# A transformer of eight stages on one core: the two-layer experts' routing done per group, partly inside the last attention slot

## The reference, cut to what matters

```python
x = x + tanh(g_xattn[2]) * L2_xattn(layernorm(x), ctx)   # stage 4: 16 heads
x = x + tanh(g_ffn[2])   * L2_ffn(layernorm(x), ...)     # stage 5: 8 experts, one per token
x = x + tanh(g_xattn[3]) * L3_xattn(layernorm(x), ctx)   # stage 6: one head, weights rounded

def _L2_ffn_ref(x, Wr, br, W1, b1, W2, b2):              # D 256, F 1024, 8 experts
    expert_idx = argmax(x @ Wr.T + br)
    h = relu(x @ W1[e].T + b1[e]);  y = h @ W2[e].T + b2[e]     # for e = expert_idx
def _quantize_kernel(kern):                              # on Wq and Wk of stage 6
    s = 2 * max(|kern|) / 256;  return round(kern / s) * s
```

## Time and profile before

| what | value |
|---|---|
| median of 3 runs | 1383.21 us (1383.08 to 1385.77) |
| the profiled execution | 1370.34 us, span 1368.6 us |
| PE busy, of the span | 1205.5 us (88%) |
| DVE busy | 702.4 us (51%) |
| ACT busy | 448.4 us (33%) |
| POOL busy | 292.8 us (21%) |
| mean granted TensorE clock | 0.924 |
| DMA | 186.75 MB, of it 102.06 MB written to HBM |

### The profile page before, as it was taken

One profiled execution on the slowest core, in us unless ns is written; L12 is line 12 of the kernel. 1 busy time (PEld: TensorE's weight loads), 2 busy tenths in 40 slices (PEclk: granted clock), 3 DMA queues, 4 the chain that ended last, 5 costly groups with the idle time before them and its releaser, 6 DMA issues.

```text
span 1368.6 us, 19327 instructions
## 1 busy us (share of the span) xinstructions
PE 1205.5 (88%) x6360; PEld 761.6 (56%) x6361; DVE 702.4 (51%) x1997; ACT 448.4 (33%) x842; POOL 292.8 (21%) x347
## 2 busy tenths in 40 slices
PE   6999999999879999999988669999667699999993
PEld 4534434434434454445334559999556545888862
DVE  7273474478876545654552521111276752455557
ACT  3322222233445354544434113333243201333320
POOL 2111111130030011010100041111123563255560
PEclk9999999999988999999888579999877789999997
DMA  9999999200000000001000845555309322555538
GB/s 301 338 336 327 334 333 333 81 14 1 0 1 1 1 1 1 1 1 34 1 0 1 270 161 194 171 182 186 114 29 349 115 89 92 144 162 166 168 111 314
DMA packets 140489, 186.75 MB, mean 136 GB/s; under 512 B 8737, under 2 KB 124961, under 8 KB 140289
## 3 DMA queue, kind: packets, MB, share of 16 engines
q1 hardware_dynamic: 130864, 159.28, 37.5%
q0 software_dynamic: 9552, 26.52, 5.3%
HBM read 83.71 MB, written 102.06 MB: 136 GB/s over the span
## 4 chain that ended last, share of the span: by engine, by line
PE 74%; DVE 13%; ACT 4%; issue 3%; DMA 3%; POOL 2%; SPq 0%; POOLq 0%; DVEq 0%; ACTq 0%
PE psum L2005 13%; PE psum L1266 6%; PE psum L1277 6%; PE psum L1055 6%; PE psum L2217 5%; PE psum L1074 3%; PE psum L936 3%; PE psum L2274 3%; PE psum L1995 2%; PE psum L2251 2%; PE psum L2298 2%; PE psum L2195 2%; PE psum L2034 2%; DVE arena L2836 2%; PE psum L947 2%
## 5 line engine op out<-in xcount | busy, mean ns | idle before, releaser
L2005 PE MATMUL psum<-arena 128*128 128x512 f32 x432 | 199.6, 604 | 0.0
L2836 DVE TENSOR_REDUCE arena<-psum 128x4 f32<-128x616 f32 x128 | 101.5, 796 | 98.6 <-PE psum L2217 97.3
L2005 PEld LDWEIGHTS psum<-arena 128*128 128x128 f32 x432 | 77.7, 190 | 102.8 <-issue 102.0
L2217 PE MATMUL psum<-arena 32*128 32x308 f32 x512 | 104.0, 498 | 16.9 <-DVE arena L2836 16.0
L1182 POOL DMA_INDIRECT ys<-xnT,arena x96 | 92.1, 959 | 90.9 <-DVE xnT L1159 68.4
L2418 ACT ACTIVATE arena<-psum,arena 128x512 f32<-128x512 f32 x72 | 49.0, 685 | 160.4 <-PE psum L2005 150.7
L1894 POOL TENSOR_TENSOR x_tok<-x_tok,add_row 128x1024 f32<-128x1024 f32 x16 | 38.3, 2400 | 266.6 <-ACT xn L1759 266.5
L2509 ACT ACTIVATE arena<-psum 128x2048 f32<-128x2048 f32 x40 | 75.0, 1874 | 60.1 <-PE psum L2255 41.6
L1266 PEld LDWEIGHTS psum<-side,arena 128*128 128x128 f32 x736 | 87.8, 196 | 2.7 <-ACT side L1311 1.6
L1055 PE MATMUL psum<-arena,xn 128*128 x384 | 87.1, 380 | 2.4 <-ACT xn L1105 1.9
L1266 PE MATMUL psum<-side,arena 128*128 128x128 f32 x736 | 88.2, 279 | 1.0 <-ACT side L1311 1.0
(11 more groups left out here) (418 smaller groups left out, 2090.4 us busy)
## 6 DMA issues: line engine op xcount, KB each, us to landing
xs<-zeros SPq DMA_DIRECT2D x8, 8576.0 KB, 60.0
arena<-in_W SPq DMA_DIRECT2D x31, 1024.0 KB, 5.0
xn<-xs SPq DMA_DIRECT2D x64, 134.0 KB, 2.4
arena<-in_gate_up SPq DMA_DIRECT2D x4, 2048.0 KB, 15.9
arena<-xs SPq DMA_DIRECT2D x32, 134.0 KB, 2.3
arena<-in_down SPq DMA_DIRECT2D x4, 1024.0 KB, 14.6
arena<-ys SPq DMA_DIRECT2D x4, 1024.0 KB, 12.5
arena<-ys SPq DMA_DIRECT2D x2, 2048.0 KB, 14.0
```

What stands on the lines that cost most here:

```text
L2005: ins = pe.matmul(bank[dict(hn=4, r=5, z=6, xn=7)[k]][:], lhs[:, cols], r, start=(start and n == 0), stop=(stop and n == len(w) - 1))
L2217: ins = pe.matmul(bank[most_bank(n, k) + i][:, 0:2 * M].rearrange("p (h m) -> p h m", h=2), qhT[rows, n % 3, c, t * P:(t + 1) * P], keys[r ...
L2836: dve.tensor_reduce(neg[:, n % 2, t, 2 * pair:2 * pair + 2, 2 * c:2 * c + 2], psum[:, most_bank(n, k):most_bank(n, k) + 2, 0:2 * M].rearra ...
```

## The change

Each expert of stage 5 gets a fixed region of 16 tiles in xs5, which grows to 129 tiles (128 and one that stays zero). A token's row is 2048 times its expert plus its rank, so it needs no counts of later groups: `hot5_vector`, `ranks5_tensor` and `slots5_vector` work group by group, and POOL sends a group as soon as its rows are known. The 23 tiles that the experts work on are found at the end (`tiles_vector`, `passed_vector`, `rows5_vector`, shared with stage 7 or new), and SP reads each tile's first row from a register before its load. In `flow()` groups 0 and 1 are turned, routed and ranked inside slot 7, and group 2's turn and logits stand there too; group 3 comes after. The rest of group 2's norm moves from between the `untangle`s of slot 7 to behind group 0's places. The maxima of stage 6's weights are taken between group 2's experts and its places, the rounding after the tile list; PE's key product no longer waits for that list. The weights of stage 6 and six of the eight W2 loads are issued earlier.

```diff
+E2, F2 = 8, 1024
+REGION = T
-SPARE = E4 * REGION
+SPARE, SPARE5 = E4 * REGION, E2 * REGION
...
-            yield from (("back", n, 0), ("back", n, 1), ("project", n, 0), ("project", n, 1))
+            yield from (("back", n, 0), ("back", n, 1), ("r_turn", 2), ("project", n, 0), ("project", n, 1), ("r_logits", 2))
...
             yield ("weigh", n, 4)
+            yield from routed("r_turn", 0)
...
             yield from late("late_turn")
+            yield from routed("r_logits", 0)
...
             yield from behind("project", n - 1, 1)
+            yield from routed("r_turn", 1)
...
             yield ("values", n, 1)
+            yield from routed("r_ranks", 0)
...
             yield ("weigh", n, 2)
+            yield from routed("r_logits", 1)
...
             yield ("values", n, 3)
+            yield from routed("r_ranks", 1)
...
+        def slots5_vector(dve, ch, g):
+            r = route[5]
+            dve.wait_ge(*ranks_done.at(5, g + 1))
+            ch.step(dve.scalar_tensor_tensor(r["place"], iota_e[:, 0:E2].unsqueeze(1).broadcast_to([P, GT, E2]), float(REGION * P),
+                                             bank[5][:, 0:GT * E2].rearrange("p (t e) -> p t e", t=GT), ALU.mult, ALU.add))
...
+        def scatter_gpsimd(pool, g):
+            pool.wait_ge(*slots_ready.at(5, g + 1))
...
+            for t in range(GT):
+                pool.indirect_dma_start(xs5, bass.IndirectOffsetOnAxis(route[5]["slot_i"][:, g * GT + t, 0:1].bitcast(U32), 0),
+                                        xn[:, g, t, 0:D5], None).then_inc(scattered.sem, 16)
...
             def load(i, u):
-                sp.dma_start(xin[:, u], xs5[bass.ds(i * P, P), :]).then_inc(in_loaded[u].sem, 16)
+                row = sp.value_load(first_row5[0:1, bass.ds(i, 1)], min_val=0, max_val=SPARE5 * P)
+                sp.dma_start(xin[:, u], xs5[bass.ds(row, P), :]).then_inc(in_loaded[u].sem, 16)
...
+                elif op[0] == "r_logits":
+                    if op[1] == 2:
+                        finish(5)
+                    hot5_vector(dve, ch, op[1])
+                    if op[1] == 2:
+                        single_max_vector(dve, ch)
+                elif op[0] == "r_ranks":
+                    slots5_vector(dve, ch, op[1])
+                    if op[1] == 0:
+                        finish(5)
...
-                sp.wait_ge(*x_done.at(4, G))
                 for k, name in enumerate(("wk6", "wv6", "wq6")):
+                    if k != 1:
+                        sp.wait_ge(*emptied(("values", SLOTS - 2 + k // 2, 3)))
...
-                for e in range(E2):
+                for e in (0, 1, 4, 5, 6, 7, 2, 3):
+                    if e == 2:
+                        sp.wait_ge(*x_done.at(4, G))
...
             if last_stage >= 5:
-                route_vector(dve, ch, 5, br5)
+                slots5_vector(dve, ch, G - 2)
+                hot5_vector(dve, ch, G - 1)
+                slots5_vector(dve, ch, G - 1)
+                tiles_vector(dve, ch, 5)
+                passed_vector(dve, ch, 5)
+                rows5_vector(dve, ch)
+                single_round_vector(dve, ch)
                 single_context_vector(dve, ch)
```

More of the change, by code:

```diff
@@ L326, in part @@
                 return r if dt is F32 else r.bitcast(dt)
-            TT = T if s_ == 5 else GT
+            TT = GT
             route[s_] = dict(
@@ new lines, in turn5_tensor @@
+        def turn5_tensor(pe, g):
+            pe.wait_ge(*xn_ready.at(5, g + 1))
+            if g == 0:
+                pe.wait_ge(most_found, 16 * SLOTS)
+            elif g == 1:
+                pe.wait_ge(*logits_read.at(5, 1))
+            elif g == 2:
+                pe.wait_ge(*logits_read.at(5, 2))
+                pe.wait_ge(*slots_ready.at(5, 2))
+            else:
+                pe.wait_ge(weighed, weighed_at[SLOTS - 1, 3] + 1)
+            for c in range(C):
+                for t in range(GT):
+                    ins = pe.transpose(bank[(2 if g == G - 1 else 4) + c][:, t * P:(t + 1) * P], xn[:, g, t, c * P:(c + 1) * P], ident[:])
+                ins.then_inc(turned.sem, 1)
@@ new lines, in copy5_scalar, with logits5_tensor @@
+        def copy5_scalar(act, g):
+            if g >= 2:
+                act.wait_ge(*logits_done.at(5, g - 1))
+            copy_turned(act, 5, g, xnT[:, g % 2], 2 if g == G - 1 else 4)
+        def logits5_tensor(pe, g):
+            if g == 0:
+                pe.wait_ge(w5_loaded, 4 * 16)
+            else:
+                pe.wait_ge(*logits_read.at(5, g))
+            pe.wait_ge(*xnT_ready.at(5, (g + 1) * C))
+            for t in range(GT):
+                for c in range(C):
+                    ins = pe.matmul(bank[4][:, t * E2:(t + 1) * E2], xnT[:, g % 2, c, t * P:(t + 1) * P], wr5[:, c],
+                                    start=(c == 0), stop=(c == C - 1))
+            ins.then_inc(logits_done.sem, 1)
@@ new lines, in ranks5_tensor @@
+        def ranks5_tensor(pe, g):
+            r = route[5]
+            pe.wait_ge(*hot_ready.at(5, g + 1))
+            pe.wait_ge(*earlier_ready.at(5, 1 + GT * (g + 1)))
+            if g == 0:
+                pe.wait_ge(*xnT_ready.at(5, 2 * C))
+            else:
+                pe.wait_ge(*slots_ready.at(5, g))
+            if g == G - 1:
+                pe.matmul(bank[5][0:E2, 128:129], r["earlier"][:, T], ones_bf[:, 0:1], start=True, stop=True)
+            for t in range(GT):
+                dst = bank[5][:, t * E2:(t + 1) * E2]
+                pe.matmul(dst, before[:], r["hot"][:, t, 0], start=True, stop=False)
+                ins = pe.matmul(dst, ones_bf[:], r["earlier"][:, g * GT + t], start=False, stop=True)
+            ins.then_inc(ranks_done.sem, 1)
```

293 lines of the change are left out of this document (131 added, 162 removed).

## The result

The changed kernel took 1369.72 us (median of 7, 1367.27 to 1376.32) against 1385.45 (7 runs, 1382.68 to 1392.18) for the kernel before: ratio 0.9896, 95% interval 0.9871 to 0.9921. By that ratio it is 14.4 us less (10.9 to 17.9); the two medians differ by 15.7. Forecast: 10.3 less, 1372.9, range 1366 to 1380.

The account below looks back on a forecast made before the run. The bound was taken as one 55.0 us chain from stage 4's last addition to the experts' first turn. 9.9 - 20.8 - 2.4 + 3.0 = -10.3 us gave 1360.0 profiled, 1372.9 as median, range 1366 to 1380.

Parts of the forecast that it names:

- The stall in slot 7: PE idles 5 us before `rests` of rows 2 and 3, waiting for DVE; `rests` starts at 751.4, +10.2.
- The clock: Slot 7: PE's clock falls to 1.2 GHz in the 5 us idle, then recovers; +3 us.
- rival 1: Clock stays down in slot 7: +8.5 in place of +3, giving 1378; 18 in 100.
- the slot: Slot 7 grows by 12.9 us, of which 9.9 before the clock term and 3.0 for the clock.
- The routing tail: Slot 7's end to experts' start: 34.2 us, not 55.0, by a 22.9 us chain and 11.3 of context; -20.8.
- Rival 2: POOL's sends stay last before the experts, start 0 to 3.5 us later, giving 1375; 8 in 100.
- the 2 to 6: Before the experts: the context is last, 2 to 6 us after the rows loaded from xs5.
- the last send's landing: End of routing: POOL's last send, at 786.6, lands 2.44 us later.
- The warm start: Experts' first tile: with PE warm, its first layer takes 3.57 us instead of 6.00; -2.4.
- Zeroing and register reads: Start and experts' loop: zeroing runs 42 us longer, register reads delay each load under 1 us; both cost zero.
- The sum: Whole kernel: 9.9 - 20.8 - 2.4 + 3.0 = -10.3 us, profiled execution from 1370.3 to 1360.0.
- the 12.9 us between profile and median: Whole kernel: the runs' median lies 12.9 us above the profiled execution; the same difference again gives 1372.9.

Follow-up runs that it names:

- experiment 3: Changed kernel with 32 unread transposes on PE ahead of `rests` of rows 2 and 3 in slot 7: ratio 0.9916 to the kernel before.
- experiment 7: Changed kernel with the first eight context matmuls issued twice; trace only: norm of group 3 to experts' first turn 35.1 us instead of 33.2.
- experiment 5: Changed kernel with POOL waiting for the last group's places before its first send, routing left early: ratio 0.9967 to the kernel before.
- experiment 6: Kernel before with only xs5 enlarged to 129 tiles and all of it zeroed: ratio 0.9987 to the kernel before.
- experiment 12: Changed kernel, unchanged, measured again beside the kernel before on one chip: 1359.63 us against 1370.91, ratio 0.9926.
- experiment 1: Changed kernel with group 2's norm back where it was and its turn behind the last projection: ratio 0.9889 to the kernel before.
- 4: Changed kernel with all four groups' routing behind slot 7, still group by group: ratio 0.9939 to the kernel before.
- experiment 8: Changed kernel with two unread POOL products ahead of group 3's sends; trace only: experts' first turn 4.1 us later.
- experiment 2: Changed kernel with group 2's norm as one block behind slot 7's second division (rows 1): ratio 0.9877 to the kernel before.
- `warm`: experiment 2 with stage 6's clears and two maxima moved into DVE's idle time, plus unread transposes in PE's waits after slot 7: ratio 0.9905.

## Why the prediction came out right

**The stall in slot 7.** `rests` was forecast for 751.4 and started at 750.74, with a stall of 4.61 us where 5 was forecast, by the mechanism named: places, norm, search, two divisions on DVE while PE idles.

**The clock.** Forecast +3.0, measured 2.6 (experiment 3). It fell in the stall and came back within the slot; rival 1, that it stays down, did not happen. Together the slot grew by 11.1 (11.3 on the one chip), forecast 12.9: 0.7 of the 1.8 too much lay ahead of `rests`, 0.4 in the clock.

**The routing tail.** Forecast 34.2, measured 33.2. In it two errors partly cancel: DVE's chain up to the context's matmuls took 21.5 and not 22.9 us, the context 11.7 and not 11.3, because its first matmuls ran longer at the lower clock (4.30 against 3.88). DVE is in the chain throughout and the context is last (experiment 7). Rival 2, sends last, did not happen; it does with all 16 sends at the end (experiment 5). The rows have about 2.8 us to spare by the estimate above, within the 2 to 6; their load was issued at 793.60, while I had the last send's landing 2.44 behind it. It landed some 6 us behind it, while the DMAs moved 373 to 385 GB/s: that term was too small, and harmless.

**The warm start.** Forecast -2.4, measured -2.2: the first layer went from 6.00 to 3.84. The 3.57 of the forecast was a later tile's share of the chain; the second tile took 3.84 before and after. All together the experts' end moved from 980.1 to 967.1, 13.0 earlier.

**Zeroing and register reads.** Forecast zero. For the zeroing experiment 6 (by its interval at most 0.02% slower) and the iteration's busy time show it; that the register reads cost nothing was only seen (the first layers follow each other as before).

**The sum** was -10.3. The stages give -12.8 by the first two traces and -13.0 by the two of one chip: 1.8 too much in the slot, 0.9 too little in the tail, 0.2 too much for the warm start. By the times it is -14.4 (-10.9 to -17.9) in the first measurement and -10.1 (-7.1 to -13.0) in experiment 12, and the two intervals overlap. **What was right by luck**: I added the 12.9 us between profile and median as if any run carried them. By the traces such a gap is what stage 7 shows in nine profiles and lacks in five; that the first profile and its runs differ by it is inferred. On the chip without it the kernel takes 1359.6, and my sum for the profiled execution was 1360.0.

**What I had wrong** in testing it: that moving the norm would save its stall (experiment 1), and that the routing in the slot is worth almost nothing (4).

The Trainium skill (TensorE: Matmul & The Clock Gate, "Part 1: The HAM clock gate") has idleness halve the clock: the 0.99 to 0.50 above agrees. The skill's port rule (SBUF — State Buffer, "SBUF: two separate sides") says that a GpSimd instruction and a VectorE instruction in a two-port mode exclude each other for a whole instruction. The 4.25 us of experiment 8 agree in size, though not on who comes first: L771's record begins 0.42 us ahead of POOL's first product, and it lasts through both. That L771 ran in such a mode no run shows. The page's further step, that VectorE keeps GpSimd from writing the descriptors of its DMAs, hardly shows: in the changed kernel sends follow one another every 1.26 to 1.28 us behind the first pair (1.51), beside DVE's work too, and only in experiment 5 did two take 1.06 and 1.14 us instead of 0.96.

## What to carry to other kernels

Work moved under a busy stretch costs more than its own length if it sits on the engine that feeds that stretch: here one block of 5 us on DVE became most of a PE stall of 4.61 us, and then 2.6 us of slower clock. Behind the next division (experiment 2) the same block cost two short stalls and no clock, 3.7 us less by the trace. Shorter stalls alone are no guarantee: in experiment 1 the clock fell behind one of 2.37 us. So place such a block where the feeding engine has the largest lead, and check what PE runs next if the clock drops. When a queue at the end is cut (here POOL's sends), find out what is last next: 16 sends became 8, and only 8.3 of 21.7 us are theirs. And when a profile and a median disagree by more than the change is worth, compare by stages, and profile both kernels on one chip.

## What the runs showed that I had not expected

- The clock can fall while PE is busy: in `warm` it fell at 770, with PE busy for all but 0.2 us since 768, after it had been busy for 0.6 to 0.8 of each 2 us from 764 to 768.
- Two POOL products of 1.90 us each and one small DVE instruction (L771) of 4.25 us end within 0.1 us of each other; in nine other profiles, some with POOL's indirect DMAs (0.96 us each) beside it, the same instruction takes 0.27 to 0.40 us.
- The kernel before takes 1371 us on one chip and 1385 to 1389 in the other sets. Two of its profiles, one of them with zeroing, differ by 16.8 us behind the experts' first turn (557.5 against 574.3), most of it waits of stage 7 for its loads.
